# Dealing 49 degree lookups over pieces 8 to 86 instead of 1 to 86 of a graph network's first adjacency stream

## The reference, cut to what matters

```
x = layernorm(x + L0(x))      # sum over neighbours, two dense layers
x = layernorm(x + L1(x))      # four convolutions, norm = dinv[src] * dinv[dst]
x = layernorm(x + L2(x))      # edge features, see below
x = layernorm(x + L3(x))      # two convolutions with mean over neighbours

# in L2
edge_norm = (norm[src] * norm[dst])[:, None]
msg = edge_norm * (h[src] + efeat @ We + be)
agg = segment_sum(msg, dst)
```

## Time and profile before

| | |
|---|---|
| median of 3 runs | 2728.84 us (2728.23 to 2730.37) |
| the profiled execution | 2729.3 us, span 2727.5 us |
| TensorE busy | 2580.1 us |
| VectorE, ScalarE, GpSimd busy | 1488.3, 613.4, 156.5 us |
| mean granted TensorE clock | 0.991 |

### The profile page before, as it was taken

The page is one execution under the profiler, slowest core; times in us unless marked ns, Lnnn a source line. Parts: engine busy times, 40 slices in busy tenths (PEclk is TensorE's granted clock), DMA queues, the critical chain, the costliest instruction groups (busy, mean ns, idle before and its releaser), DMA issues.

```text
span 2727.5 us, 42004 instructions
## 1 busy us (share of the span) xinstructions
PE 2580.1 (95%) x16397; PEld 1478.7 (54%) x16397; DVE 1488.3 (55%) x5515; ACT 613.4 (22%) x737; POOL 156.5 (6%) x113
## 2 busy tenths in 40 slices
PE   2879999957999999999999999999999999999998
PEld 0657666733555555556555555555555555555555
DVE  6999999867777666666656623333222221112222
ACT  2768888760000011111111100000000000000000
POOL 3000000002000011111111100000000200000000
PEclk9999999988999999999999999999999999999999
DMA  6225222225767655555555555454554454545554
GB/s 162 77 71 75 93 94 94 105 76 169 221 207 221 186 175 174 173 172 171 172 180 169 148 150 185 138 139 136 139 138 136 136 136 138 138 137 155 151 151 115
DMA packets 233638, 395.59 MB, mean 145 GB/s; under 512 B 42298, under 2 KB 214158, under 8 KB 229976
## 3 DMA queue, kind: packets, MB, share of 16 engines
q1 hardware_dynamic: 203728, 326.08, 42.0%
q10 hardware_dynamic: 28904, 64.79, 7.3%
q0 software_dynamic: 800, 1.94, 0.2%
HBM read 343.43 MB, written 49.32 MB: 144 GB/s over the span
## 4 chain that ended last, share of the span: by engine, by line
PE 77%; DVE 18%; DMA 1%; ACT 1%; DVEq 1%; issue 1%; SPq 0%; ACTq 0%; POOL 0%; POOLq 0%
PE PS L1575 71%; DVE S L899 8%; DVE S L898 6%; PE PS L1760 1%; DMA XN<-in_x_dram 1%; PE PS L1767 1%; PE PS L1768 1%; PE PS L1782 1%; DMA HR<-adjacency 0%; PE PS L1765 0%; PE PS L1791 0%; PE PS L1764 0%; PE PS L1714 0%; PE PS L1740 0%; ACT XN L1391 0%
## 5 line engine op out<-in xcount | busy, mean ns | idle before, releaser
L1575 PE MATMUL PS<-HR,HN 128*128 128x500 fp8e3 (+1 forms) x5096 | 1061.3, 366 | 2.4 <-issue 1.9
L1575 PE MATMUL PS<-HR,AGN 128*128 128x500 fp8e3 (+1 forms) x4606 | 926.1, 350 | 3.2 <-DMA HR<-adjacency 3.1
L1575 PEld LDWEIGHTS PS<-HR,HN 128*128 128x128 f16 x5096 | 489.8, 97 | 517.2 <-issue 5.7
L1575 PEld LDWEIGHTS PS<-HR,AGN 128*128 128x128 f16 x4606 | 445.0, 97 | 391.1 <-issue 6.1
L1575 PE MATMUL PS<-S 128*128 128x245 f16 x1250 | 336.5, 276 | 43.1 <-DVE S L899 38.7
L899 DVE TENSOR_SCALAR S<-S,RBW 128x245 f16<-128x245 f16 x1250 | 341.5, 273 | 0.0
L1081 DVE TENSOR_SCALAR AT<-PS,SC 128x384 f32<-128x384 f32 (+24 forms) x100 | 43.2, 472 | 513.1 <-PE PS L1575 496.4
L898 DVE TENSOR_SCALAR S<-iot,RBW 128x128 f16<-128x128 f16 x1250 | 297.4, 238 | 2.3 <-PE PS L1575 1.7
L1575 PEld LDWEIGHTS PS<-S 128*128 128x128 f16 x1250 | 120.0, 97 | 166.7 <-issue 40.5
L1230 DVE TENSOR_SCALAR TB<-iot,dstF 128x208 f16<-128x208 f16 x833 | 159.1, 270 | 5.9
L677 POOL TENSOR_TENSOR AT<-AT,dstI 128x1088 f32<-128x1088 f32 x49 | 100.6, 2053 | 827.1 <-DVE mxe L1204 827.1
(11 more groups left out here) (241 smaller groups left out, 1821.6 us busy)
## 6 DMA issues: line engine op xcount, KB each, us to landing
HR<-adjacency SPq DMA_DIRECT2D x588, 437.5 KB, 3.5
AT<-source_lanes ACTq DMA_DIRECT2D x49, 544.0 KB, 5.2
AT<-in_edge_attr_dram ACTq DMA_DIRECT2D x48, 544.0 KB, 4.6
adjacency<-HN SPq DMA_DIRECT2D x9, 1531.2 KB, 5.5
adjacency<-HR SPq DMA_DIRECT2D x8, 1531.2 KB, 5.7
adjacency<-TB SPq DMA_DIRECT2D x8, 1531.2 KB, 5.6
HR<-adjacency SPq DMA_DIRECT2D x49, 218.8 KB, 2.5
edge_rows<-AT ACTq DMA_DIRECT2D x8, 416.0 KB, 12.6
```

The source lines that it names most:

```text
L1575: return t_.matmul(out_, w, m, start=start, stop=True, skip_group_check=True)
```

## The change

`LOOK_AT` says at which piece of pass 1 each of the 49 lookups stands. Before, the first stood at piece 1, and 85 steps were dealt among 48 gaps (1, 2, 4, 6, 8, 9, 11, 13, ...); now the first stands at piece 8 and 78 steps are dealt (8, 9, 11, 12, 14, 16, 17, ...). The last stands at piece 86 in both. `LOOK_AT` is read by TensorE (`lookup`), VectorE (`degrees`) and ScalarE (`lanes`) alike. Nothing else changes.

```
-        LP = [1 + g * (PCS - 6) // (NG - 1) for g in range(NG)]
+        LP = [PIECES + 1 + g * (PCS - PIECES - 6) // (NG - 1) for g in range(NG)]
         LOOK_AT = {n: g for g, n in enumerate(LP)}
```

## The result

The changed kernel takes 2707.18 us (median of 4 runs, 2706.51 to 2709.38) against 2728.97 of the kernel before: a ratio of 0.9921, with a 95% interval of 0.9904 to 0.9938. That is 21.8 us less. The profiled execution took 2707.39 us with a span of 2705.6 us, and TensorE's busy time is unchanged (2579.8 us against 2580.1). A slow matmul counts as busy, so what was gained is idle time; the time on the slow clock is about the same in sum.

The account below looks back on a forecast made before the run. TensorE, busy 95% of the span, was taken as the bound, so only its idle and slow-clock time could go. 28.3 us removed less 2.0, 6.9 and 2.2 added gave 17.2 us less: 2711.6 us, range 2705 to 2717.

Parts of the forecast that it names:

- Rival B: VectorE's `bounds` not held by GpSimd: stall before lookup 1 only 3.9 us, clock kept, 22.4 us gained, 2706.4 us; chance 0.27.
- The long wait, its slow restart and the two early stalls: TensorE's idle before lookup 0, slow matmuls behind it, stalls before lookups 1 and 5: 23.74, 2.2 and 1.75 us removed.
- The wait for piece 6's low half: In the first unit, TensorE waits for VectorE's low half for piece 6: 2.0 us added.
- The stall before lookup 1: TensorE waits near 632 for VectorE, which does `sums`, `lengths` and `bounds` of unit 0 first: 6.9 us added.
- `bounds` against GpSimd: VectorE's two-input instructions in `bounds` get through only when GpSimd's additions end; the other reading was 3.0 us smaller.
- The slow restart behind it: Slow clock after the wait before lookup 1: 2.2 us added; a 3.9 us wait would not pay it.
- The pairs behind the rows' piece: Stalls where a lookup follows one at a piece of remainder 3 by 7: two remain (25, 74), 0.65 us less.
- Pass 1 in sum: All removed and added terms around the first stream together: 17.2 us less.
- The later passes have no clock of their own; what is gained here stays: After pass 1, the old timeline merely shifts, keeping the gain unchanged.
- C: Backlog behind `bounds`: lookups 2 to 5 also stall, another 2 to 5 us, 2714 to 2717 us; chance 0.16.
- D: Denser deal makes VectorE the bound: 0.65 us at each of 47 later lookups, 13.4 us slower, 2742 us; chance 0.02.
- E: Pieces 2 to 6 wait for something else up to 627; time within 0.2% of 2728.8 us; chance 0.03.

Follow-up runs that it names:

- e1: Kernel before, with the lookups dealt from piece 4 on instead of piece 1: 2715.94 us, ratio 0.9956.
- e11: Changed kernel, unchanged, timed a third time on the same chip as two other variants: 2707.97 us, ratio 0.9924.
- e8: Changed kernel, unchanged, run once more for its trace: 2707.65 us.
- e5: Changed kernel with GpSimd's seven residual additions placed behind its 49 products: 2711.59 us, ratio 0.9932.
- e3: Changed kernel with GpSimd's seven residual additions held back until lookup 20 is emptied: 2706.68 us, ratio 0.9922.
- e9: Changed kernel with GpSimd's additions behind its products and after VectorE's last edge group's one-hot tiles and low halves: 2702.55 us, ratio 0.9901.
- e2: Kernel before, with GpSimd's seven residual additions held back until lookup 20 is emptied: 2725.43 us, ratio 0.9988.
- e6: Changed kernel with the same first four lookups, the others re-dealt to make more pairs behind the rows' piece: 2720.84 us, ratio 0.9968.
- e4: Changed kernel with VectorE's `bounds` moved from piece 7 to behind the degrees of piece 9: 2708.06 us, ratio 0.9927.
- e10: Changed kernel with the first lookup at piece 10 instead of 8: 2703.11 us, ratio 0.9908.
- e7: Kernel before, unchanged, run once more for its trace: 2730.37 us.

## Why the prediction was right, point by point

The forecast was 2711.6 us in a range of 2705 to 2717; 2707.2 lies in it, and 21.8 us less came where 17.2 were forecast. The part that the sum was about, pass 1, agrees within 1.1 us; the other 3.5 us were not forecast, so most of the 4.6 us between 17.2 and 21.8 lies outside the mechanism. Rival B's figure (2706.4) is nearer, but its mechanism did not happen.

- *The long wait, its slow restart and the two early stalls* (23.74 + 2.2 + 1.75): gone, all three. e1 shows the cause by a dose: three pieces put before the lookup take 8.35 us from the wait. I had priced the stalls by their idle time; from start to start this part and the one pair less cost 0.6 us more than the 28.3.
- *The wait for piece 6's low half*: 2.0 forecast, and 2.0 lost in the first unit. The half came when forecast, 19.7 us behind the stream's start. As a wait it stands only in traces with a start at full clock (2.05 us in e11); in the first trace and in e8 most of it is a slow start, which the forecast did not have and which costs nothing here, because the half is not there earlier.
- *The stall before lookup 1*: 6.9 forecast, 6.24 found (4.65 in e11, where piece 6 was slow). The forecast counted from the end of GpSimd's additions. They took 15.45 us where I had 15.8 (0.4 of the difference), and the rest of `bounds` took 2.6 behind them and not 2.8. There were six VectorE turns among them again and not four, but they cost GpSimd 1.2 us in sum, where the six before had cost 2.4. `sums` and `lengths` took 2.73 us (625.00 to 627.73) and not 3.24, which did not matter, since `bounds` had to wait for GpSimd anyway.
- *`bounds` against GpSimd*: taken at the dear end, and rightly. 3.1 us more than alone (5.9 against 2.86), where 3.0 was the difference of my two ends. That the one-element, one-input instructions of `bounds` would pass was not put to the test, since they came after the additions (the like instructions of e5 did pass, 0.15 us beside them); two of three two-input ones wait for an addition, as line 1191 and the Trainium skill (SBUF — State Buffer, Who interferes with whom) had it, while line 1032 passed right behind line 1031 in every trace with the additions there; e3, e5 and e9 show the same lines at 0.15 without GpSimd. Rival B is refuted.
- *The slow restart behind it*: 2.2 forecast, 1.8 found. That a wait of 3.9 us would not have paid it had no row, and the runs speak against it: slow matmuls follow waits of 4.65 us (e11), 4.00 (e2), 2.88 (e3) and some of 2.0 to 2.7. Rival B's 22.4 us rest on this too.
- *The pairs behind the rows' piece*: two stalls of 0.65 us idle at pieces 25 and 74 as forecast, and e6 buys more at the same price, which is 0.90 from start to start. That pieces 35, 56 and 77 lose 0.28 each was not foreseen.
- *Pass 1 in sum*: 17.2 forecast, 18.3 found by the means, 18.1 in the first two traces. The stall gave 0.7 back, the restart 0.4 and the removed stalls 0.6; the three unforeseen places took 0.8.
- *"The later passes have no clock of their own; what is gained here stays"*: this step is not borne out, to the good. 1.6 us more came at the start of pass 2, where the kernel before restarts slowly behind a wait of 2.7 us and the changed one does not, and about 2 us in the start of the stream. Of the first I can say where it is and that it came in all five traces of the two kernels, not why these kernels differ; no run separated it from the position of the matmuls before it. Of the second, the traces of all variants scatter by 5 us, and five traces of the two kernels are too few to call it an effect of the change.
- *Rivals C, D, E*: C's backlog did not come; lookups 2 to 5 have no listed stall in the changed kernel. D's denser deal costs only at its pairs, and E is refuted by e1.

## What to carry to other kernels

Where engines run in order, a step with slack belongs behind the work that its inputs can still hide under: look not at the step's cost but at what is queued behind it, and at when its input can be there at the earliest. Here, moving it once exposed the next late input (VectorE's `bounds`, slowed by GpSimd), and a little further along (piece 10 and not 8) that one was covered too, for one changed constant. GpSimd's work without a deadline should stand where VectorE runs neither its tiles nor two-input masks; two of three new places gave back what the first had cost.

## What was not expected of the hardware

- Two-input VectorE instructions of a single element a partition wait for the GpSimd addition that is running (1.33 and 2.04 us for 0.15; an addition alone takes 2.04), though one right behind another that had waited passed (line 1032, 0.15), while one-input instructions of the same size pass (line 1210 in the earlier trace rows, and again in e5 at 1536.64, beside the additions: 0.15).
- Size matters for one-input instructions: those of one element pass (0.15), a cast of 49 elements (2.06 us for 0.18) and a tile of 208 or 2176 do not.
- A wait of about 2 us before piece 6 was followed by a slow piece in e4, e6 and e11 (4.78, 4.78 and 4.82 us for 3.12) and not in e5 and e10 (3.13, behind 2.05 and 1.83). The start of the stream, behind a similar idle time, was slow in the first trace of the changed kernel, e2, e3, e7, e8 and e9, and at full clock in the others. Stretches in e11 before and behind its start at 614.58, and in e5 behind its start at 616.44 (columns as above):

```profile
606.00:614.50 8.50, 6.53 (x31) 2.65 (x29) 4.11 (x16) 5.97 (x19) 0.00 (x0) 1.00 0.50 132
614.60:618.00 3.40, 3.40 (x12) 1.34 (x13) 1.89 (x2) 1.23 (x4) 2.83 (x2) 0.68 0.96 269
```

```profile
616.50:619.50 3.00, 3.00 (x16) 1.40 (x17) 1.27 (x3) 1.23 (x4) 0.00 (x0) 1.00 1.05 344
```

The clock was 1.00 up to the wait in e11 and lower behind it (0.68 over 3.4 us, the lower level being 1.2 GHz), and 1.00 behind the same wait in e5. So the length of a short wait alone does not say what it costs; 1.6 to 1.8 us come and go with it.
